# Scores of two batches from unsplit float32 q and k, and modulation products in another place

## The reference

```python
mod = (silu(c) @ wmod).reshape(32, 6, 1, 128)
sa, ca, ga, sb, cb, gb = (mod[:, n] for n in range(6))
ga = (2 * (ga >= 0) - 1) * maximum(abs(ga), 0.25)
gb = (2 * (gb >= 0) - 1) * maximum(abs(gb), 0.25)
h = layernorm(x) * (1 + ca) + sa
q, k, v = split((h @ w_in.T + b_in).reshape(32, 256, 16, 24), 3, axis=-1)
att = softmax(einsum('blhd,bmhd->blmh', q, k) / sqrt(8), axis=2)
opt = einsum('blmh,blhd->blhd', att, v).reshape(32, 256, 128)
x = x + ga * (opt @ w_out.T + b_out)
h = layernorm(x) * (1 + cb) + sb
# logits = h @ router_w; the best of 14 experts per token, gelu MLP 128-256-128, weighted by its softmax
x = x + gb * expert_output
```

## Time and profile before

| what | value |
|---|---|
| median of 3 runs | 610.16 us (607.28 to 612.15) |
| span of the profiled execution | 609.1 us, 12013 instructions |
| busy: DVE, ACT, POOL, PE | 91%, 90%, 80%, 77% of the span |
| granted TensorE clock, mean of the span | 0.632 of 2.4 GHz |
| first exponential | 22.26 us |

### The profile page before, as it was taken

The page is one execution under the profiler, slowest core; times in us unless marked ns, Lnnn a source line. Parts: engine busy times, 40 slices in busy tenths (PEclk is TensorE's granted clock), DMA queues, the critical chain, the costliest instruction groups (busy, mean ns, idle before and its releaser), DMA issues.

```text
span 609.1 us, 12013 instructions
## 1 busy us (share of the span) xinstructions
PE 471.5 (77%) x2535; PEld 266.9 (44%) x2537; DVE 555.4 (91%) x1419; ACT 545.2 (90%) x2323; POOL 484.3 (80%) x642
## 2 busy tenths in 40 slices
PE   5456887877887777788788788778776688989993
PEld 2113433333343333333334343334333366889992
DVE  5898999999999999999999999999999978788884
ACT  2599999999999999999999999999999963767882
POOL 4566777998999989899998989989898765677763
PEclk9555556566556756655655655675555565999997
DMA  6365544544455555555555555665555215888750
GB/s 194 104 189 157 138 140 125 139 138 140 141 149 148 148 152 140 163 142 167 146 156 149 148 154 148 173 172 145 160 149 152 93 65 143 269 281 255 223 180 27
DMA packets 77072, 94.42 MB, mean 155 GB/s; under 512 B 12806, under 2 KB 60710, under 8 KB 76998
## 3 DMA queue, kind: packets, MB, share of 16 engines
q1 hardware_dynamic: 68842, 75.69, 45.0%
q0 software_dynamic: 6144, 16.82, 7.4%
q10 hardware_dynamic: 2015, 1.15, 0.7%
HBM read 58.41 MB, written 35.20 MB: 154 GB/s over the span
## 4 chain that ended last, share of the span: by engine, by line
ACT 48%; POOL 17%; DVE 12%; PE 11%; issue 8%; DMA 2%; ACTq 1%; POOLq 0%; DVEq 0%; SPq 0%
ACT scores L927 47%; DVE neg_max L1395 4%; PE scores L1223 4%; PE scores L1232 4%; POOL table L838 3%; POOL xhat L787 2%; POOL rstd L770 2%; POOL rest L577 2%; POOL parts L580 2%; POOL h_scaled L810 1%; DVE y_biased_s L1966 1%; DMA table<-rows,place_i 1%; PE scores L1213 1%; POOL xhat L779 1%; POOL att L799 1%
## 5 line engine op out<-in xcount | busy, mean ns | idle before, releaser
L927 ACT ACTIVATE scores<-scores,neg_max 128x256 f32<-128x256 f32 x1024 | 468.5, 827 | 10.5 <-DVE neg_max L1395 10.4
L927 ACT ACTIVATION_READ_ACCUMULATOR scores<-scores,neg_max 128x1 f32 x1024 | 436.2, 588 | 0.0
L1395 DVE TENSOR_REDUCE neg_max<-scores 128x4 f32<-128x1024 f32 x256 | 309.2, 1211 | 7.5 <-PE scores L1073 7.0
L1073 PE MATMUL scores<-k_stack,q_stack 64*128 64x256 bf16 x1024 | 148.5, 389 | 79.3 <-ACT scores L927 67.7
L1073 PEld LDWEIGHTS scores<-k_stack,q_stack 64*128 64x128 bf16 x1024 | 34.0, 106 | 164.3 <-ACT scores L927 120.6
L838 POOL DMA_INDIRECT table<-rows,place_i x64 | 66.0, 1031 | 20.4 <-issue 17.0
L787 POOL TENSOR_SCALAR xhat<-rows,mv,rstd 128x128 f32<-128x128 f32 x60 | 47.6, 796 | 7.1 <-POOL rstd L770 7.1
L893 POOL DMA_INDIRECT out_dram<-x_s x40 | 39.4, 986 | 17.4 <-DVE x_s L1977 9.2
L1232 PE MATMUL scores<-w_s,hid 128*128 x308 | 49.8, 286 | 2.2 <-DVE y_biased_s L1966 1.1
L1101 PE MATMUL side_a<-w_gated,opt_t 128*128 128x128 f32 x128 | 49.7, 491 | 0.0
L779 POOL TENSOR_SCALAR xhat<-x_s,mv,rstd 128x128 f32<-128x128 f32 x62 | 49.1, 801 | 0.4 <-POOL rstd L770 0.4
(11 more groups left out here) (231 smaller groups left out, 876.0 us busy)
## 6 DMA issues: line engine op xcount, KB each, us to landing
q_stack<-parts_dram SPq DMA_DIRECT2D x192, 64.0 KB, 2.9
x_s<-table SPq DMA_DIRECT2D x62, 192.5 KB
parts_dram<-parts SPq DMA_DIRECT2D x31, 384.0 KB, 3.0
k_stack<-parts_dram SPq DMA_DIRECT2D x186, 64.0 KB, 2.2
mod_b<-mod_rows SPq DMA_DIRECT2D x32, 256.0 KB, 4.4
x_s<-in_x_dram SPq DMA_DIRECT2D x13, 256.0 KB, 4.8
table<-pad_tile SPq DMA_DIRECT2D x15, 192.5 KB
more_rooms<-table SPq DMA_DIRECT2D x15, 192.5 KB
```

The lines of the kernel that those rows point to most:

```text
L927: last = act.activation(buf[:, k * L:k * L + L], buf[:, k * L:k * L + L], ACT.Exp, bias=neg_max[:, p, n:n + 1], accum_out=exp_sum[:, p, n: ...
L1073: last = pe.matmul(scores[:, c, at:at + L], q_stack[p][r, g + j, t * P:t * P + P], k_stack[p][r, g + j, :], start=True, stop=True)
L1395: dve.tensor_reduce(to, scores[:, (PAIRS * b.n + i) % RING, :].rearrange("p (e j m) -> p e j m", e=2, j=2), AX_X, ALU.max, negate=True).th ...
```

## The change

Batches 0 and 1 (`DIRECT = 2`) get no parts, no stores and no stacks. Their q and k are projected with the unpermuted weights `w_qkv_s`, which leaves four heads in each strip of 32 partitions. For each of the four places in a strip a copy of q is made in which all other heads are zero (`q_masked`: scale by a mask, add a masked bias), and a score product takes 32 partitions of such a copy and of `k_plain`, in float32. For batch 0 ScalarE makes the four copies and VectorE adds k's bias, for batch 1 VectorE does both (`take_plain`). The buffers lie in the room of the expert weights w2, which are loaded much later. The masks come from the identity by two reductions and two scalings on VectorE, ahead of the permuted weights.

The late modulation becomes two separate products, one ahead of the turn of batch 0 and one behind its q and k, into `side_b`; ScalarE copies each. The first `modulate` goes ahead of batch 0, the other and `modulate_rest` into batch 0; `gated_bias` goes to GpSimd ahead of its iterations. On each engine the work of the start for batches 1 and 2 (`turn_x`, `make_h`, `stats_x`) and the projection of batch 1 move in between the score pairs of batch 0 (`first_iteration`). Five small loads go from ScalarE's queue to SP's; the x of batches 4 to 7 is loaded ahead of batch 0; in SP's iteration 0 `store_parts` of batch 2 goes behind the loads of the modulation row and of x and the padding.

```diff
+DIRECT = 2
+STRIP = 32
+IN_STRIP = STRIP // DH
...
         def split_by(eng, steps, b):
-            eng.wait_ge(qk_ready, b.done())
-            need(eng, parts_stored, 16 * b.n - 16)
-            if b.n == 2:
-                eng.wait_ge(first_k_stored, 16)
+            eng.wait_ge(qk_ready, b.n - DIRECT + 1)
+            need(eng, parts_stored, 16 * (b.n - DIRECT - 1))
...
             sp.wait_ge(pad_set, 1)
             pad_front(0)
-            sp.wait_ge(stacks_set, 4)
-            sp.wait_ge(first_q_ready, 1)
-            sp.dma_start(parts_dram[0, 0].rearrange("s r t -> r s t"), parts[:, 0, 0]).then_inc(parts_stored, 16)
-            sp.wait_ge(parts_stored, 16)
-            steps.plain()
-            load_stacks_by(sp, 0, (0,))
-            store_parts(Batch(1))
-            parts_landed(Batch(1))
-            load_stacks_by(sp, 1, (0, 1))
             load_x(3)
...
                 if b.ago(-2).there():
                     parts_landed(b.ago(-2))
-                    sp.wait_ge(scored, PAIRS * b.n + PAIRS)
+                    if b.n >= DIRECT:
+                        sp.wait_ge(scored, PAIRS * b.n + PAIRS)
+                    else:
+                        sp.wait_ge(stacks_set, 4)
                     load_stacks_by(sp, b.slot(2), (0, 1))
...
+            take_mod(0)
+            act.wait_ge(masks_ready, 1)
             act.wait_ge(first_q_done, 1)
...
+            for i in range(IN_STRIP):
+                act.activation(q_masked[0][:, i, :], first_qk[0], ACT.Identity, bias=strip_bias[:, i:i + 1],
+                               scale=strip_mask[:, 1, i:i + 1]).then_inc(q_masked_ready, 1)
+            take_mod(1)
             over_batches(iteration, drain)
...
+            def score_plain(b, i):
+                c = (PAIRS * b.n + i) % RING
+                if b.n == 0:
+                    pe.wait_ge(k_plain_ready, 1)
+                    pe.wait_ge(q_masked_ready, 2 + i % 2 * 2)
+                    pe.wait_ge(b_taken, 1)
+                elif i == 0:
+                    pe.wait_ge(k_plain_ready, 2)
+                need(pe, exped, PAIRS * b.n + i - RING + 1)
+                t, g = i // 4, i % 4 * 2
+                for j in range(2):
+                    for e in range(2):
+                        head = e * HALF + g + j
+                        r = slice(head // IN_STRIP * STRIP, head // IN_STRIP * STRIP + STRIP)
+                        at = e * 512 + j * L
+                        last = pe.matmul(scores[:, c, at:at + L], q_masked[b.n][r, head % IN_STRIP, t * P:t * P + P],
+                                         k_plain[b.n][r, :], start=True, stop=True)
+                last.then_inc(scored, 1)
...
+            dve.wait_ge(b_qk_loaded, 16)
+            steps.then(dve.tensor_reduce(own_head[:, :], ident_s[:, :].rearrange("p (h d) -> p h d", d=DH), AX_X, ALU.max))
+            steps.then(dve.tensor_reduce(strip_mask[:, 0, :], own_head[:, :].rearrange("p (r i) -> p i r", i=IN_STRIP), AX_X, ALU.max))
+            steps.then(dve.tensor_scalar(strip_mask[:, 1, :], strip_mask[:, 0, :], SCALE, None, ALU.mult))
+            dve.tensor_scalar(strip_bias[:, :], strip_mask[:, 1, :], b_qk_s[:, 0, 0:1], None, ALU.mult).then_inc(masks_ready, 1)
...
+            def take_plain(b):
+                dve.wait_ge(qk_done, b.done())
+                dve.wait_ge(masks_ready, 1)
+                steps.plain()
+                steps.then(dve.tensor_copy(q_plain, side_b[:, 0:L]))
+                for i in range(IN_STRIP):
+                    dve.tensor_scalar(q_masked[b.n][:, i, :], q_plain, strip_mask[:, 1, i:i + 1], strip_bias[:, i:i + 1],
+                                      ALU.mult, ALU.add)
+                dve.tensor_scalar(k_plain[b.n], side_b[:, L:2 * L], b_qk_s[:, 0, 1:2], None, ALU.add).then_inc(k_plain_ready, 1)
```

More of the change, by code:

```diff
@@ L327, in build_adaln_attention_moe @@
         b2_s = sb("b2_s", [P, E, D])
+        w2_room = w2_s[:, :, :, :].rearrange("p e f d -> p (e f d)")
+        q_masked = [w2_room[:, n * IN_STRIP * L:(n + 1) * IN_STRIP * L].rearrange("p (i t) -> p i t", t=L) for n in range(DIRECT)]
+        plain = w2_room[:, DIRECT * IN_STRIP * L:(DIRECT * IN_STRIP + DIRECT + 1) * L].rearrange("p (n t) -> p n t", t=L)
+        k_plain = [plain[:, n, :] for n in range(DIRECT)]
+        q_plain = plain[:, DIRECT, :]
         expert_s = sb("expert_s", [P, 3, E])
@@ L686, in iteration @@
                     sp.dma_start(bias_dram.rearrange("r (b d) -> b r d", d=D), bias_out[:, :, :]).then_inc(bias_stored, 16)
-                if b.ago(-2).there():
+                if b.n > 0 and b.ago(-2).there():
                     store_parts(b.ago(-2))
@@ L845, in _ @@
             normalise_x(Batch(2))
-            split_by(pool, steps, Batch(1))
             pool.wait_ge(w_in_loaded, 16 * LOADS_IN)
+            gated_bias()
             def iteration(b):
@@ L1034, in _, with late_mod @@
             last.then_inc(mod_done, 1)
-            def late_mod():
+            def late_mod(n):
                 pe.wait_ge(wmod_late_loaded, 16)
-                for n in range(2):
-                    last = pe.matmul(scores[0:B, 0, n * 512:n * 512 + 3 * D], silu, wmod_s[:, n * 3 * D:(n + 1) * 3 * D], start=True, stop=True)
-                last.then_inc(mod_done, 1)
+                need(pe, mod_taken, n)
+                pe.matmul(late_mod_p, silu, wmod_s[:, n * 3 * D:(n + 1) * 3 * D], start=True, stop=True).then_inc(mod_done, 1)
             def turn_x(b):
@@ L1060, in project_k, with project_plain @@
                 pe.matmul(side_b[:, L:2 * L], w_qk_s[:, 1, :], h_t[b.slot(RING_H)][:, :], start=True, stop=True).then_inc(qk_done, 1)
+            def project_plain():
+                pe.wait_ge(h_ready, 2)
+                pe.wait_ge(mod_taken, 2)
+                for n in range(2):
+                    last = pe.matmul(side_b[:, n * L:n * L + L], w_qkv_s[:, n, :], h_t[1][:, :], start=True, stop=True)
+                last.then_inc(qk_done, 1)
+            def score_plain(b, i):
+                c = (PAIRS * b.n + i) % RING
+                if b.n == 0:
+                    pe.wait_ge(k_plain_ready, 1)
[13 more added lines that the diff above has]
+                last.then_inc(scored, 1)
             def score(b, i):
+                if b.n < DIRECT:
+                    score_plain(b, i)
+                    return
                 p, c = b.slot(2), (PAIRS * b.n + i) % RING
                 if i == 0:
-                    pe.wait_ge(stacked[p], 16 * LOADS_STACK * b.earlier(2) + 16 * LOADS_STACK)
+                    pe.wait_ge(stacked[p], 16 * LOADS_STACK * b.earlier(2))
                 need(pe, exped, PAIRS * b.n + i - RING + 1)
@@ L1554, in _, with x_stats_of @@
             dve.wait_ge(b_taken, 1)
[L1555 to L1573 removed]
+            def take_plain(b):
[7 more added lines that the diff above has]
+                dve.tensor_scalar(k_plain[b.n], side_b[:, L:2 * L], b_qk_s[:, 0, 1:2], None, ALU.add).then_inc(k_plain_ready, 1)
+            def x_stats_of(b):
+                stats_x(b)
+                dve.wait_ge(xhat1_ready, b.n)
+                steps.plain()
+                means(True, False)
             def modulate(n):
@@ L1694, in early_done, with first_iteration @@
                                                                   op0=ALU.mult, op1=ALU.add))
+            def first_iteration(b):
+                row_max(b, 0)
+                make_h(Batch(1))
+                row_max(b, 1)
+                x_stats_of(Batch(2))
+                row_max(b, 2)
+                dve.wait_ge(mod_taken, 2)
+                steps.plain()
+                modulate(1)
+                row_max(b, 3)
+                take_plain(Batch(1))
+                row_max(b, 4)
+                make_h(Batch(2))
+                x_stats_of(Batch(3))
+                row_max(b, 5)
+                modulate_rest()
+                row_max(b, 6)
+                take_qk(Batch(2))
+                row_max(b, 7)
+                prepare_ranks()
             def iteration(b):
+                if b.n == 0:
+                    first_iteration(b)
+                    return
                 ahead, fresh = b.ago(-2), b.ago(-3)
@@ L1728, in iteration @@
                     make_h(ahead)
-                if b.n == 0:
-                    modulate(1)
                 row_max(b, 3)
@@ L1768, in iteration @@
                     prepare_rows()
-                if b.n == 0:
-                    gated_bias()
-                elif ahead.there():
+                    prepare_below()
+                if ahead.there():
                     take_qk(ahead)
```

144 lines of the change are left out of this document (63 added, 81 removed).

## The result

The changed kernel takes 612.94 us at the median of 20 runs (610.45 to 614.98), the kernel before 609.96 beside it; the ratio is 1.0053 with a 95% interval of 1.004 to 1.0065. So it is 3 us slower, inside the range and near the 611.5 of the forecast. One of the 20 runs of the kernel before took 1481.55 us; the other 19 lie between 607.28 and 612.15, so the median hardly feels it. The profiled execution has a span of 611.9 us, 2.8 above that of before.

What follows compares the result with a forecast made beforehand. ScalarE's exponential stream bounds the kernel; q and k of batch 2 at 32.3 plus 20.4 of stack chain give 52.7 against 51.37, +1.3 us: span 609.1 to 610.4, median 611.5, range 607 to 617.

Steps and rivals of the forecast that it cites:

- The start: Work up to the first exponential: it was to start at 17.5 instead of 22.26 us, 4.7 us gained.
- The pair: Four float32 score products of 32 rows on TensorE, partly overlapping: 2.13 us at 1.2 GHz, 1.07 at 2.4.
- strips in a row: Rival: float32 strip products don't overlap, a pair costs 3.41 us at 1.2 GHz, 1.71 at 2.4; 612.5 to 618.4 us; chance 0.12.
- The 610.4 that went with it: Time in us forecast if strip products overlap in perfect pairs on TensorE, 1.71 us a pair at 1.2 GHz.
- VectorE in batch 0: VectorE's work from first row maximum to q and k of batch 2: 13.9 us; 3 to 3.5 us of ScalarE waits.
- TensorE in batch 0: TensorE's work in batch 0, at changing clock, was to move q and k of batch 2 from 31.4 to 32.3.
- The chain of the stacks: Splitting, storing and loading from q and k of batch 2 to its exponentials: 20.4 us, bounds 19.1 to 21.4.
- both levels in turn: TensorE's clock was to alternate between 1.2 and 2.4 GHz during strip products, costing a little under a third of 3.5 us.
- the rival in which the clock stays at 1.2: TensorE bounds batches 0 and 1 at the low clock; batch 2 starts at 58.9, +7.5, 617.7 us; chance 0.09.

Runs made afterwards that it cites:

- bf16 strips: Changed kernel with q's masked strips and k of batches 0 and 1 kept in bf16 instead of float32; 606.30 us, ratio 0.9944 to the kernel before.
- the second (32.53): The changed kernel run again unaltered, with a new profile; 613.65 us at the median of ten, ratio 1.0055 to the kernel before.
- the two bf16 kernels: Changed kernel with bf16 q copies and k in batches 0 and 1, without and with batch 1's masked q copies on GpSimd; 606.30 and 605.11 us.
- 64 rows: Changed kernel with strip products of batches 0 and 1 contracting over 64 rows instead of 32, computing something else; 612.52 us, ratio 1.0024 to the kernel before.
- GpSimd strips in float32: Changed kernel with batch 1's four masked strips of q scaled by GpSimd instead of VectorE, still float32; 613.96 us, ratio 1.0049 to the kernel before.
- early q and k: Changed kernel with batch 2's q and k taken after batch 0's fourth row maximum, ahead of batch 1's strips; 618.27 us, ratio 1.0135 to the kernel before.

## Why the prediction was right in time and wrong in a step

**The start** went as forecast: first strip product 14.14 (13.9), first exponential 17.53 (17.5), turn of x at 9.39 (9.15).

**The pair** was set at 2.13 and 1.07 us by the clock. It takes 2.08 and 1.13 with its draining. Where two pairs on the same strips follow each other, the second adds 1.71 (3.79 less 2.08, at 48.20 in the changed kernel), and the next product starts 3.71 behind the first (51.91), so 1.86 a pair. The reason for 2.13, that only the second half of a product overlaps the next, is out with it: 1.71 is the four steps of 0.43 of perfect pairs. Out as well are strips in a row, at 3.4. The Trainium skill's rule in TensorEngine Tiling (Array Packing), Theoretical Speedup, up to 4x for a contraction of 32, is the better one. The trace agrees: a second pair on the same two strips adds the 1.71 that the prediction drew from that rule, and 16 instructions of two pairs on four strips took 2.10, as long as 8. The 610.4 that went with it didn't come, since the price of a pair wasn't the only thing on TensorE's row.

**VectorE in batch 0**, 13.9 us from the first row maximum to q and k of batch 2, measured 13.7 with bf16 strips, where nothing else binds; the 3 to 3.5 us of holes are 3.2 there. The strips of batch 1 cost 2.5 us for the 2.45 worked out.

**TensorE in batch 0** was given 0.9 us on q and k of batch 2 (32.3 instead of 31.4). It took 2.3 in the first profile (33.74), 1.1 in the second (32.53), with the clock low throughout in the one and up until 25.4 in the other.

**The chain of the stacks**, 20.4 us with 19.1 as its lower bound, is 19.1 and 19.5 in the two bf16 kernels, where it binds (29.93 to 49.05, 28.36 to 47.90). With 64 rows it is 18.5 (33.29 to 51.77), below the bound, with no hole ahead of batch 2.

**The step that failed** is "ScalarE is through with batches 0 and 1 at 17.5 + 28.8 + 3.5 = 49.8, so the stacks bind and nearly 3 us of hole open there". It gave batch 1 the 14.4 us of ScalarE alone. Batch 1 lasts 17.44, and TensorE's row is full at 1.2 GHz in it (busy for 13.58 of 13.90 us from 38.0 to 51.9). The stacks had landed at 50.34, ahead of the 53.06 at which the first product reads them. There is no hole ahead of batch 2; ScalarE waits 2.6 us inside batch 1 instead, three times, for row maxima. I had expected "both levels in turn"; in the traces of the changed kernel batch 1 runs at the low one. That is the rival in which the clock stays at 1.2, with the mark that was named for it ("if TensorE's row in batches 0 and 1 is full at 0.50, or if batch 2 waits for nothing"). Its own price was too high, 58.9 for batch 2 and 617.7 us: 16 pairs at 1.86 instead of 2.13 are 4.3 us less, which covers the 3.7 between 58.9 and 55.20.

So the time came out between two stories, and that it lay in the range is luck as far as the mechanism goes: a rival with a chance of 0.09 came true at half its price (3.8 us at batch 2 instead of 7.5). Against the forecast of 52.7 at batch 2 the fault is 2.5 us. The prize that was missed is as large: without TensorE's bound the change is worth 2.3 us at batch 2 (51.37 to 49.05, bf16 strips), and with VectorE's strips taken off as well 3.5 (47.90), both with rounded scores.

**What stays open** is what decides the clock. It was high in batch 1 in one trace of 64-row products and low there in all of 32 rows in float32, of which two were of the same kernel; one trace against several isn't enough to lay it to the rows.

## What to carry to other kernels

A wait that ends in the start is worth only what the engines behind it can use: before trading loads for products, add up each engine's row over the batches that are hit, at both clock levels, and compare with the engine that binds, here 14.4 us a batch. An edit that relieves an engine that isn't the last bound gives nothing (GpSimd strips in float32: 0.01 us at batch 2) and can give something once the bound is gone (1.15 with bf16), so try it again afterwards; relieving a chain that isn't the bound can even cost (early q and k, 5 us). Work that partly fills a wait at the start (1.8 us for 2.8) can cost its whole length and more where it is moved into a full row (4.3 in batch 0).
